# Rotated operands in one buffer, their low parts ahead of the next rotation, and an earlier k weight, in a four-layer kernel

## What is computed

```python
# layer 1 (tag b_): biases, no rotation
q = (norm(x) @ Wq + bq); k, v = split(ctx @ Wkv + bkv)
x = x + softmax(q k^T / sqrt(128)) v @ Wo + bo
# layer 3 (tag d_): rotation and a causal mask, no biases
q, k = rope(norm(x) @ Wq.T), rope(ctx @ Wk.T);  v = ctx @ Wv.T
x = x + softmax(mask(q k^T / sqrt(128))) v @ Wd.T
# rope(t) = t * cos + concat(-t2, t1) * sin, over the halves t1, t2 of a head's 128 columns
```

## Time and profile before

| | us |
|---|---|
| median of 3 runs | 2114.82 |
| lowest, highest | 2111.25, 2125.43 |
| the profiled execution's own time | 2114.82 |
| span in its profile | 2112.7 |
| busy in the span: TensorE matmul / VectorE / ScalarE / POOL | 1807.0 / 1504.1 / 1072.4 / 1038.2 |
| layer b steady, first to last scores | 257 to 874 |
| layer d, first to last scores | 1222 to 1822 |

### The profile page before, as it was taken

One profiled execution on the slowest core, in us unless ns is written; L12 is line 12 of the kernel. 1 busy time (PEld: TensorE's weight loads), 2 busy tenths in 40 slices (PEclk: granted clock), 3 DMA queues, 4 the chain that ended last, 5 costly groups with the idle time before them and its releaser, 6 DMA issues.

```text
span 2112.7 us, 26355 instructions
## 1 busy us (share of the span) xinstructions
PE 1807.0 (86%) x8645; PEld 1468.2 (69%) x8645; DVE 1504.1 (71%) x2735; ACT 1072.4 (51%) x2556; POOL 1038.2 (49%) x889
## 2 busy tenths in 40 slices
PE   5664799999999999774967689999999999878879
PEld 3443677788788788662744568888888888656757
DVE  6667489989989985547343578888888888747740
ACT  2433477777777775422334245555555543335630
POOL 3665265655655654413132257776776742016720
PEclk7997899999999999966866799999999999989989
DMA  3002111111121120020002011111111110111120
GB/s 114 6 1 77 45 41 50 61 51 46 55 61 46 46 65 16 23 84 1 0 1 75 25 31 51 36 36 51 36 42 45 36 50 1 42 30 50 38 69 35
DMA packets 53991, 88.00 MB, mean 42 GB/s; under 512 B 8992, under 2 KB 15648, under 8 KB 53600
## 3 DMA queue, kind: packets, MB, share of 16 engines
q1 hardware_dynamic: 53856, 86.33, 13.6%
HBM read 75.56 MB, written 10.75 MB: 41 GB/s over the span
## 4 chain that ended last, share of the span: by engine, by line
PE 30%; DVE 21%; issue 16%; POOLq 11%; POOL 8%; ACT 6%; DVEq 5%; DMA 1%; SPq 0%; ACTq 0%
POOLq L326 7%; PE c_ps L66 7%; DVE b_st_u L253 6%; POOLq L324 4%; PE a_ps L66 3%; PE d_ps_job L66 3%; PE e_ps L66 3%; PE b_ps_o L66 3%; DVEq L254 3%; PE b_ps_job L66 3%; POOL d_roped L1018 2%; PE d_ps_o L66 2%; ACT b_st_sign L234 1%; POOL c_cs L1532 1%; PE d_ps_s L66 1%
## 5 line engine op out<-in xcount | busy, mean ns | idle before, releaser
L66 PE MATMUL b_ps_o<-b_wo,b_oT 128*128 128x512 f32 x768 | 191.4, 397 | 18.5 <-DVE b_oT L1260 18.5
L66 PE MATMUL d_ps_o<-d_wo,d_oT 128*128 128x512 f32 x768 | 192.0, 399 | 9.9 <-DVE d_oT L1259 9.8
L66 PE MATMUL b_ps_job<-xnT,b_wq 128*128 128x512 f32 x768 | 192.0, 403 | 3.8 <-DVE b_qT L1260 3.2
L1018 POOL TENSOR_TENSOR d_roped<-d_rot_a,d_rot_b 128x512 f32<-128x512 f32 x80 | 104.7, 1308 | 184.2 <-DVE d_rot_b L1269 184.2
L66 PE MATMUL d_ps_job<-xnT,d_wq 128*128 128x512 f32 x768 | 192.6, 403 | 0.1
L323 POOL TENSOR_SCALAR b_pt_sign<-b_pt_sign 128x512 f32<-128x512 f32 x112 | 79.8, 712 | 210.7 <-ACT b_pt_sign L315 200.4
L253 DVE SCALAR_TENSOR_TENSOR b_st_u<-b_st_sign,b_st_u 128x512 f32<-128x512 bf16 x182 | 176.5, 970 | 9.1 <-issue 0.4
L66 PEld LDWEIGHTS b_ps_o<-b_wo,b_oT 128*128 128x128 f32 x768 | 142.5, 187 | 57.3 <-DVE b_oT L1260 24.3
L66 PEld LDWEIGHTS d_ps_o<-d_wo,d_oT 128*128 128x128 f32 x768 | 144.3, 190 | 47.9 <-DVE d_oT L1259 15.2
L66 PEld LDWEIGHTS b_ps_job<-xnT,b_wq 128*128 128x128 f32 x768 | 144.4, 193 | 35.0 <-issue 5.5
L66 PEld LDWEIGHTS d_ps_job<-xnT,d_wq 128*128 128x128 f32 x768 | 143.1, 191 | 31.1 <-PE c_ps L66 0.5
(11 more groups left out here) (366 smaller groups left out, 4505.2 us busy)
## 6 DMA issues: line engine op xcount, KB each, us to landing
b_raw<-in_wq_dram SPq DMA_DIRECT2D x32, 256.0 KB, 2.6
b_raw<-in_wo_dram SPq DMA_DIRECT2D x32, 256.0 KB, 2.8
d_raw<-in_wq_dram SPq DMA_DIRECT2D x32, 256.0 KB, 2.6
d_raw<-in_wo_dram SPq DMA_DIRECT2D x32, 256.0 KB, 2.7
e_nat<-dequantized SPq DMA_DIRECT2D x30, 256.0 KB, 3.0
b_st_v<-in_quantized_dram SPq DMA_DIRECT2D x13, 256.0 KB, 3.0
dequantized<-b_st_u SPq DMA_DIRECT2D x13, 256.0 KB, 2.8
a_ctx_in<-in_ctx_dram SPq DMA_DIRECT2D x8, 256.0 KB, 5.2
```

Source lines behind the costliest of these rows:

```text
L66: i = pe.matmul(out, a, b, start=first and t == 0, stop=last and t == len(terms) - 1)
L1018: pool.tensor_tensor(roped[:, n % 2], rot_a[:], rot_b[:], ALU.add).then_inc(s_sum, 1)
```

## The change

The order of `WEIGHTS` puts k third, so that it is loaded earlier, and its high and low parts are made at step 1 of half A instead of step 3, in both attention layers. `roped` becomes one buffer. A rotated operand's high and low parts are both made in the step of its rotation: the first q's copy moves ahead of the code tile's signs on ScalarE and its low part ahead of the second rotation on VectorE (at i = 0, where there is no second rotation, it stays behind the residual add). The second operand's copy and low part move to the end of the same step, behind those of `oT`. POOL's second sum waits for the low part of the first operand instead of an earlier one, since it overwrites the only buffer.

```diff
-    WEIGHTS = [("q", 0), ("q", 1), ("q", 2), ("q", 3), ("k", 0), ("v", 0), ("o", 0), ("o", 1), ("o", 2), ("o", 3)]
+    WEIGHTS = [("q", 0), ("q", 1), ("k", 0), ("q", 2), ("q", 3), ("v", 0), ("o", 0), ("o", 1), ("o", 2), ("o", 3)]
...
-            roped = sb("roped", [P, 2, HALF, P])
+            roped = sb("roped", [P, HALF, P])
...
-            return at(N_BATCH * (g - 1) + (HALF + j if kind == "o" else j if kind == "q" else 3), 9.6)
+            return at(N_BATCH * (g - 1) + (HALF + j if kind == "o" else {"q": j, "k": 1, "v": 3}[kind]), 9.6)
...
         def gpsimd(pool):
-            def rope_sum(n, read, n_read):
-                pool.wait_ge(s_rot, n + 1)
+            def rope_sum(n_before, read, n_read):
+                pool.wait_ge(s_rot, n_before + 1)
                 pool.wait_ge(read, n_read)
-                pool.tensor_tensor(roped[:, n % 2], rot_a[:], rot_b[:], ALU.add).then_inc(s_sum, 1)
+                pool.tensor_tensor(roped[:], rot_a[:], rot_b[:], ALU.add).then_inc(s_sum, 1)
...
                     r = rots_before(c)
-                    rope_sum(r, dve_q, max(0, q_before(c) - (i < 2)))
+                    if i == 2:
+                        rope_sum(r, dve_kv, kv_before(c))
+                    else:
+                        rope_sum(r, dve_q, q_before(c))
                     if i > 0:
                         yield at(c, 6.2)
-                        if i == 1:
-                            rope_sum(r + 1, dve_q, q_before(c))
-                        else:
-                            rope_sum(r + 1, dve_kv, kv_before(c))
+                        rope_sum(r + 1, dve_q, q_before(c) + 1)
...
                     low(weight(g, "q", i))
+                    if i == 1:
+                        low(weight(g, "k"))
                     if i == 3:
-                        low(weight(g, "k"))
                         low(weight(g, "v"))
...
         def scalar(act):
-                if jobs_at(c) and rope and i > 1:
-                    r = rots_before(c) - 1
-                    act.wait_ge(s_sum, r + 1)
-                    if i == 2:
-                        act.copy(kT[nhalf][:, 0], roped[:, r % 2]).then_inc(act_kv, 1)
-                    else:
-                        act.copy(qT[nhalf][:, 0, 3], roped[:, r % 2]).then_inc(act_q, 1)
...
+                    elif q_jobs(c):
+                        act.wait_ge(s_sum, rots_before(c) + 1)
+                        act.copy(qT[nhalf][:, 0, i], roped[:]).then_inc(act_q, 1)
...
-                if q_jobs(c) and rope:
-                    yield at(c, 8.1)
-                    r = rots_before(c)
-                    act.wait_ge(s_sum, r + 1)
-                    act.copy(qT[nhalf][:, 0, i], roped[:, r % 2]).then_inc(act_q, 1)
                 yield at(c, 9.2)
                 if valid(c, 1):
                     act.wait_ge(pe_pv, c)
                     high(oT[:, 0], ps_v[:], v_bias(c)).then_inc(act_o, 1)
+                if jobs_at(c) and rope and i in (1, 2):
+                    act.wait_ge(s_sum, rots_before(c) + 2)
+                    if i == 1:
+                        act.copy(kT[nhalf][:, 0], roped[:]).then_inc(act_kv, 1)
+                    else:
+                        act.copy(qT[nhalf][:, 0, 3], roped[:]).then_inc(act_q, 1)
...
                     weight_high(weight(g, "q", i))
-                    if i == 3:
-                        weight_high(weight(g, "k"))
+                    if i in (1, 3):
                         act.wait_ge(pe_kv, kv_before(c) + 1)
-                        weight_high(weight(g, "v"))
+                        weight_high(weight(g, "k" if i == 1 else "v"))
...
         def vector(dve):
-                if jobs_at(c) and rope and i > 1:
-                    yield at(c, 2.3)
-                    if i == 2:
-                        dve.wait_ge(act_kv, kv_before(c))
-                        low(kT[nhalf][:, 1], roped[:, (rots - 1) % 2], kT[nhalf][:, 0]).then_inc(dve_kv, 1)
-                    else:
-                        q_low(q_before(c) - 1, qT[nhalf], roped[:, (rots - 1) % 2], 3)
...
                 yield at(c, 5.6)
-                if not rope:
-                    for j in q_jobs(c):
-                        q_low(q_before(c) + (j == 3), qT[nhalf], four(BANK_Q[j]), j, q_bias(c, j))
+                if i > 0 or not rope:
+                    for j in q_jobs(c)[0:1 if rope else 2]:
+                        q_low(c, j, nhalf)
...
-                if q_jobs(c) and rope:
-                    yield at(c, 8.2)
-                    q_low(q_before(c), qT[nhalf], roped[:, rots % 2], i)
+                if jobs_at(c) and rope and i == 0:
+                    q_low(c, 0, nhalf)
                 yield at(c, 9.5)
                 if valid(c, 1):
                     dve.wait_ge(act_o, c)
                     low(oT[:, 1], ps_v[:], oT[:, 0], v_bias(c)).then_inc(dve_o, 1)
+                if jobs_at(c) and rope and i == 1:
+                    dve.wait_ge(act_kv, kv_before(c) + 1)
+                    low(kT[nhalf][:, 1], roped[:], kT[nhalf][:, 0]).then_inc(dve_kv, 1)
+                if jobs_at(c) and rope and i == 2:
+                    q_low(c, 3, nhalf)
```

More of the change, by code:

```diff
@@ L1269, in rotate, with q_low @@
                 dve.tensor_tensor(rot_b[0:64], src[64:128], both(sinT, 64, P), ALU.mult).then_inc(s_rot, 1)
-            def q_low(n, dst, src, j, bias=None):
-                dve.wait_ge(act_q, n + 1)
-                low(dst[:, 1, j], src, dst[:, 0, j], bias).then_inc(dve_q, 1)
+            def q_low(c, j, nhalf):
+                dve.wait_ge(act_q, q_before(c) + (j == 3) + 1)
+                if rope:
+                    low(qT[nhalf][:, 1, j], roped[:], qT[nhalf][:, 0, j]).then_inc(dve_q, 1)
+                else:
+                    low(qT[nhalf][:, 1, j], four(BANK_Q[j]), qT[nhalf][:, 0, j], q_bias(c, j)).then_inc(dve_q, 1)
             if LOWS == "vector":
```

## The result

The kernel after takes 2140.95 us (median of 11 runs, 2134.41 to 2149.99) against 2120.29 for the kernel before on the same chip (2111.12 to 2125.43): a ratio of 1.0105, 95% interval 1.0082 to 1.013 (here and below the ratio is not that of the medians; the means are 22.4 us apart). The profiled execution took 2133.93, its span is 2132.2, 19.5 us longer than before.

The account below looks back on a forecast made before the run. Taken as bounds: TensorE in layer d, VectorE in layer b, with VectorE and POOL close behind in d. Sum: 2112.7 + 34 - 6 + 3 = 2143.7 us of span, 2.1 more for the run: 2146 us, range 2110 to 2162.

Parts of the forecast that it names:

- half A: Steps 0 to 3 of a group of eight, splitting q, k and v weights; in layer d claimed to cost 3.2 us.
- half B: Steps 4 to 7 of a group, splitting the output weights; in layer d claimed to cost 2.6 us.
- steps 1, 3: Layer d, half A: rotation of k 1.25 us late behind copy and low part; rotation of q3 at 1413.7 against 1409.90.
- Step 4: Layer d, half A: low part of `oT` at 1417.1 against 1414.52, so the output product comes 2.6 us later.
- Step 2: Layer d, half A: the k weight's split adds 1.25 us on POOL; sum of q2 comes 2.55 us later.
- Step 5: Layer d, end of half A: q3's low part ahead of the next mask and maximum; value product waits 0.6 us more.
- Clock, +3: TensorE in layer d: longer gap in half A lowers its clock; +3 us in all, between 0 and +7.
- TensorE is the bound in d: Layer d: TensorE sets the pace, with a floor of 76.2 us a group and one 1.19 us wait for `oT` above it.
- Layer b: Attention layer without rotation: only the early k weight matters, 0.9 to 1.3 us a group; -6 us, between -8 and +1.
- Half rate in both halves: Rival: gaps in half A and half B of layer d both drop TensorE's clock, +7 and +7, 2157 us; chance 0.17.
- VectorE absorbs it: Rival: POOL's code tile work goes behind the ropes, `oT` 1.3 us late in each half, 2125 us; chance 0.13.
- Faster: Rival: q2's low part leaving the way to `oT` closes TensorE's gap in d, with 8 in b: 2097 us; chance 0.09.

Follow-up runs that it names:

- x10: Kernel after with two buffers for `roped` and VectorE's first low part put behind the second rotation; 1.0038 of the kernel before.
- x1: Kernel before with only the k weight moved early (split at step 1 of half A) in both attention layers; 0.9992 of the kernel before.
- x3: Kernel after with the k weight back at step 3 in both layers, leaving the new operand order and single buffer; 1.0124 of the kernel before.
- x8: Kernel after with half A's v job computed twice in layer d where code tiles run, filling TensorE's gap; 1.0107 of the kernel before.
- x9: x2 with POOL's weight low parts in layer d kept back until the next step's first sum; 2102.85 us, 0.9942 of the kernel before.
- x2: Kernel before with the k weight moved early only in layer b, the one without rotation; 0.9976 of the kernel before.
- x7: x2 with, in layer d, the first q's low part moved behind that of `oT` on VectorE; 1.0012 of the kernel before.

## Why the prediction was right, and where its steps were wrong

The sign and the place came out, and so did the time: 2146 predicted, 2140.95 measured. The change itself was forecast half again too large: +31 us, where 20.7 were measured between the medians and 22.4 between the means. By layers it is +27.8 us in d and -7.4 in b where the text had +37 (34 and 3) and -6. That the two times lie only 5 us apart is in part luck, since the kernel before took 2120.29 us in the longer series and not the 2114.82 from which the forecast starts. It is luck too that half A was 0.8 us too low and half B 1.8 too high.

- **Rotation and low part (steps 1, 3).** Right. The second rotation is 1.19 us later against its sum where 1.25 was taken; x10, which undoes only the low part's place, brings it back. The low parts ahead of it took 0.69, without POOL beside them.
- **Step 4, output product 2.6 us later.** Right: it starts 38.50 us after half A's first scores (1379.67) instead of 35.91 (1378.66), 2.59 later, behind a gap of 3.59.
- **Step 2, the k weight.** Right in its place (sum of q2 8.70 us after that of k, 8.93 predicted) and wrong as a cost of the group: x1 has the same steady group as before with it, x3 the same as after without it.
- **Step 5, value product 0.6 later.** It did not wait: the output product ran 1.4 us longer at the lower clock. Half A grew by 4.0 (39.48 to 43.49) instead of 3.2.
- **Half B, 2.6 us.** This term was mis-sized: 0.85 (38.28 to 39.13). Relative to half A's first scores, the sum of q0 was 2.35 late (2.56 predicted), the first sign came 2.65 after it (2.6 predicted), yet q1 was only 3.3 late instead of 3.8, and q2 4.3 instead of 5.1. The output product was 4.26 late instead of 5.2, and half A's extra 0.8 was absorbed.
- **Clock, +3.** The fall is real, in every group (output products of 4.36 to 5.49 us in half A). It costs almost nothing: x8 takes it away, five groups stay and one is 0.4 us shorter.
- **"TensorE is the bound in d".** This step failed. With tiles the group is set by the ring through POOL's sums and VectorE's rotations (x8, x10); TensorE, at 76.3 of 78.1 us nearly full, mostly only waited for it. The order of before was itself 1.9 us a group above TensorE's 76.2, and x9, which touches only POOL's order in d, takes half of that. That the sum came close has a reason in part: delays of the ring reach TensorE as waits for `oT`. Counting them there charged what does not lengthen the group, half A's k weight and the clock.
- **Layer b** and **groups without tiles.** Right: 1.25 us a group (0.9 to 1.3 predicted), and 76.03 against 76.20. In b the wait for the copy of the transposed probabilities fell from 1.18 to 0.28 us, as said. The small VectorE instruction of 1.17 stayed long (1.27 after); the one ahead of it fell from 0.61 to 0.17.
- **The rivals.** "Half rate in both halves" did not come: half B's gap was 0.24. "VectorE absorbs it" did not come: POOL's order is fixed, as was held against it, and layer d grew by 27.8 us. "Faster" counted on 1.28 us less between residual and `oT`; the gap ahead of the output product grew instead, to 24.2 us in all.

What stays open: why x1's second group of layer d is 0.7 us longer than x2's; the 0.95 us of the first sign, which no run isolates; and why x9's groups stop 0.9 us above TensorE's 76.2. On the last the trace shows that POOL, without a wait ahead of half B's first sum before, waits 2.2 to 2.4 us there for VectorE, which has waited 2.05 us for ScalarE's `probT` (near 1421).

## What to carry to other kernels

When several engines are each above 70% busy, don't take the fullest as the bound: take one instruction that recurs in the loop, write down the intervals between its starts over a whole period, and see which interval an edit changes and whether a later one gives it back. An operation put between a producer's result and the next request to the same producer is paid at every turn, even if it takes only 0.7 us and fills an idle gap of its own engine. Work that can run while the ring waits (here a weight's low part on POOL during the rotation) belongs in that wait.

## What the hardware showed

- POOL's sum of two SBUF operands took 1.29 us alone and 1.80 beside VectorE's low part (x10); VectorE's low part of q took 0.69 alone and 1.81 beside POOL's weight (x7), 1.28 in the earlier trace rows. In x10 and x7 the one that started 0.04 us earlier kept its time and the other was stretched. The Trainium skill, "SBUF — State Buffer" (SBUF: two separate sides), has a VectorE instruction with two SBUF inputs and a POOL instruction that reads SBUF locking each other out of a shared port, the one that starts first holding it to its end. These rows agree in who keeps its time; the later one takes 0.14 us less than a full wait would make of it (1.94 and 1.95).
- TensorE ran part of the output product at its lower clock behind gaps of 3.59, 2.39 and 2.22 us, and not behind one of 2.06 (x10, 3.05 us) or 0.87 (x8). The gap alone doesn't decide: the same kernel, x3, kept full rate behind 2.40 us (granted clock 1.00 in 1341.40:1344.40) and lost it behind 2.39 (0.63 in 1506.81:1511.40):

```profile
1341.39 3.06 PE L66 MATMUL d_ps_o<-d_wo,d_oT 128*128 128x512 f32 x12 [2.40 <-DVE d_oT L1260]
...
1506.81 4.61 PE L66 MATMUL d_ps_o<-d_wo,d_oT 128*128 128x512 f32 x12 [2.39 <-DVE d_oT L1260]
```
